# The down products of six routed experts turned round: the weight stays in the array, the 320 slots move, and transposes bring the result back to rows

## The reference, cut to what matters

```
gates = softmax(tokens @ wg); expert_idx = argmax(gates)
capacity = int(1.25 * 2048 / 8)                       # 320
dispatched = einsum('sec,sm->ecm', dispatch, tokens)
h = relu(einsum('ecm,emf->ecf', dispatched, w1) + b1)
expert_out = einsum('ecf,efm->ecm', h, w2) + b2
combined = einsum('sec,ecm->sm', combine, expert_out)
x = layernorm(x + combined)
```

## Time and profile before

| what | us |
|---|---|
| runs, median (lowest to highest) | 1501.31 (1501.03 to 1507.2) |
| the profiled execution, its own time | 1506.99 |
| span of its profile | 1504.9 |
| PE busy in the span | 1416.1 |
| DVE, ACT, POOL busy | 985.0, 878.7, 558.7 |

### The profile page before, as it was taken

How to read it: one execution, slowest core, us unless ns; L and a number is a source line. 1 busy time by engine, 2 the same in 40 slices (tenths; PEclk the granted TensorE clock), 3 DMA queues, 4 the chain that set the end, 5 groups by cost and what they waited for, 6 DMA issues and landing times. The chain is left out here.

```text
span 1504.9 us, 28900 instructions
## 1 busy us (share of the span) xinstructions
PE 1416.1 (94%) x11047; PEld 1070.1 (71%) x11082; DVE 985.0 (65%) x2093; ACT 878.7 (58%) x1442; POOL 558.7 (37%) x727
## 2 busy tenths in 40 slices
PE   6899999999999999999999999999999999867997
PEld 4666666666668888888888888866655555447997
DVE  5677777666664546355444434487678889746896
ACT  1455666766556555464655546455547777636775
POOL 4246865521330121231222202152324444542766
PEclk8999999999989999999999999999999999978999
DMA  7778776662440211202022030245766533105451
GB/s 143 124 143 176 151 158 127 127 108 44 75 63 2 43 30 28 44 8 44 2 43 43 1 51 1 44 79 112 131 159 118 114 79 66 37 32 202 153 173 67
DMA packets 100344, 125.90 MB, mean 84 GB/s; under 512 B 7917, under 2 KB 90356, under 8 KB 97649
## 3 DMA queue, kind: packets, MB, share of 16 engines
q1 hardware_dynamic: 96496, 118.84, 39.6%
q0 software_dynamic: 1984, 4.09, 0.8%
q10 hardware_dynamic: 1728, 1.14, 0.3%
HBM read 50.89 MB, written 9.51 MB: 40 GB/s over the span
## 5 line engine op out<-in xcount | busy, mean ns | idle before, releaser
L958 ACT ACTIVATE probs<-eslot 128x1024 f32<-128x1024 f32 x188 | 192.6, 1025 | 106.9 <-PE eslot L692 103.6
L1187 DVE TENSOR_REDUCE mx<-mslot 128x4 f32<-128x1024 f32 x128 | 156.5, 1223 | 108.9 <-PE mslot L663 107.6
L1489 POOL TENSOR_SCALAR_AFFINE_SELECT probs<-probs 128x512 f32<-128x512 f32 x128 | 83.9, 657 | 348.7 <-ACT probs L956 348.3
L663 PE MATMUL mslot<-stack 48*128 48x256 f32 (+2 forms) x1110 | 163.8, 334 | 17.8 <-DMA stack<-split 12.1
L663 PEld LDWEIGHTS mslot<-stack 48*128 48x128 f32 (+1 forms) x1110 | 97.5, 188 | 104.2 <-issue 87.8
L1181 DVE TENSOR_REDUCE mx_blocks<-mslot 128x3 f32<-128x384 f32 x214 | 114.6, 553 | 62.1 <-PE mslot L663 51.6
L956 ACT ACTIVATE probs<-eslot 128x512 f32<-128x512 f32 (+1 forms) x256 | 111.7, 490 | 50.1 <-PE eslot L692 49.0
L1428 POOL TENSOR_SCALAR ave<-amv 128x2 f32<-128x2 f32 x64 | 22.7, 355 | 301.6 <-DVE amv L1101 260.9
L707 PE MATMUL bank<-probs,v 128*32 128x256 f32 (+1 forms) x2048 | 130.1, 367 | 4.0 <-POOL probs L1489 2.3
L692 PE MATMUL eslot<-stack 50*128 50x256 f32 (+1 forms) x1264 | 124.5, 275 | 4.0 <-ACT probs L958 2.2
L755 PE MATMUL bank<-hidden,l 128*128 128x256 f32 x512 | 114.8, 382 | 0.0
(11 more groups left out here) (269 smaller groups left out, 3512.2 us busy)
## 6 DMA issues: line engine op xcount, KB each, us to landing
stack<-split SPq DMA_DIRECT2D x240, 256.0 KB
w<-in_w SPq DMA_DIRECT2D x16, 1024.0 KB, 6.1
slot_rows<-hTf SPq DMA_DIRECT2D x4, 650.0 KB, 4.6
slot_rows_sb<-slot_rows SPq DMA_DIRECT2D x4, 650.0 KB, 6.2
expert_rows<-slot_rows SPq DMA_DIRECT2D x8, 260.0 KB, 2.7
hT<-in_xT SPq DMA_DIRECT2D x8, 256.0 KB, 8.6
xb<-in_x SPq DMA_DIRECT2D x8, 256.0 KB, 8.7
qk<-in_ctx SPq DMA_DIRECT2D x8, 256.0 KB, 2.9
```

The lines of the kernel that those rows point to most:

```text
L663: mm = pe.matmul(ps[:, first:first + m], queries(u, h, k)[:, qt * P:(qt + 1) * P], keys(u, h, k)[:, 0:m], start=clear, stop=clear or qt == ...
L958: e = act.activation(PR[:, k, :, :, :].rearrange("p a k q -> p (a k q)"), ps[:, :, :, :].rearrange("p a k q -> p (a k q)"), ACT.Exp, scale ...
L1187: dve.tensor_reduce(MX[:, :, :, p].rearrange("p q a -> p a q"), MSLOT[0][:, :, :].rearrange("p a (q k) -> p a q k", q=TT), AX.X, ALU.max)\
L1489: pool.affine_select(diagonal, diagonal, [[0, 2 * TT], [1, P]], ALU.is_ge, 0.0, base=0, channel_multiplier=-1)\
```

## The change

For the experts 1 to 6 (`BY_COLUMN`) the down products are made the other way round. `down_by_column`: for each half `c` of the 256 features the down weight (128 x 128 tiles) is resident and the 320 slots move, 24 matmuls a half, into one of two further PSUM banks (TURN). ScalarE copies each half to `down_T` in SBUF (`down_high`). In the next expert's loop, behind its second up step, PE turns the copy back by 6 transposes into the old banks DOWNS (`down_rows`). Experts 0 and 7 keep the old form. `combine(e, 0..2)` of these six experts moves on VectorE from the end of the loop of e into the loop of e + 1, behind the subtractions of f = 1, 2, 3, and `even(e, 0..2)` behind those of f = 4, 5, 6. The lists of GpSimd and of SyncE stay as they are. The rest of the diff deletes lines in the attention layers that belong to the steps "context high" and "context low", which the plan of steps does not contain, and to projections of layer 1 under `PARTED`, which holds units of layer 0 alone.

```diff
+    down_T = sb("down_T", [P, CC, CAP])
+    BY_COLUMN = range(1, E1 - 1)
 # tensor
+        def down_by_column(e):
+            for c in range(CC):
+                cs = slice(c * P, (c + 1) * P)
+                if e - 1 in BY_COLUMN:
+                    pe.wait_ge(*act_down_T.at(e - 1, c))
+                else:
+                    pe.wait_ge(*dve_rows.at(ST // 2 - 2 + c))
+                for f in range(FC):
+                    if c == 0:
+                        pe.wait_ge(*dve_hid.at(e, f))
+                    mm = products(TURN[c][:, 0:CAP], (w2_high[e % 2][:, f, cs], w2_low[e % 2][:, f, cs]),
+                                  (hid_high[e % 2][:, f, :], hid_low[e % 2][:, f, :]), f == 0, f == FC - 1)
+                mm.then_inc(*pe_down_T(e, c))
+        def down_rows(e):
+            for c in range(CC):
+                pe.wait_ge(*act_down_T.at(e, c))
+            for j, (c0, m) in enumerate(CH):
+                pe.wait_ge(*dve_down.at(e - 1, j))
+                for c in range(CC):
+                    mm = pe.transpose(DOWNS[j][0:m, c * P:(c + 1) * P], down_T[:, c, c0:c0 + m], ident[:, :])
+                mm.then_inc(*pe_down(e, j))
...
+                if e - 1 in BY_COLUMN and f == 1:
+                    down_rows(e - 1)
             pe.wait_ge(*dve_low.at("w2", e))
+            if e in BY_COLUMN:
+                down_by_column(e)
+                continue
 # scalar
+        def down_high(e, c):
+            act.wait_ge(*pe_down_T.at(e, c))
+            if e - 1 in BY_COLUMN:
+                act.wait_ge(*pe_down.at(e - 1, 2))
+            act.activation(down_T[:, c, :], TURN[c][:, 0:CAP], ACT.Copy).then_inc(*act_down_T(e, c))
...
                 weights_high("w1", e + 1)
...
+                if e in BY_COLUMN:
+                    down_high(e, 0)
                 weights_high("w2", e + 1)
+                if e in BY_COLUMN:
+                    down_high(e, 1)
                 gated_bias(e + 1)
 # vector
-                if e >= 1 and f in (1, 3):
+                if e == 1 and f in (1, 3):
                     even(e - 1, (f + 1) // 2)
+                if e - 1 in BY_COLUMN and f in (1, 2, 3):
+                    combine(e - 1, f - 1)
+                if e - 1 in BY_COLUMN and f in (4, 5, 6):
+                    even(e - 1, f - 4)
...
+            if e in BY_COLUMN:
+                weights_low("w2", e + 1)
+                continue
             combine(e, 0)
```

More of the change, by code:

```diff
@@ L101, in build @@
         sb = lambda name, shape: outer.enter_context(nc.sbuf_tensor(name, shape, F32))
[L102 to L105, removed]
+        shared = {"ident": sb("ident", [P, P]), "w1": sb("w1", [P, CC, DFF]), "w2": sb("w2", [P, DFF // P, C]),
+                  "spare": sb("spare", [P, 16 * KEEP])}
         for name in ("w1_in", "w2_in", "biases_in", "scattered", "base_out"):
@@ L279, in attention_layers @@
     HID_A, HID_B = hidden
-    KT_HIGH, KT_LOW = [[shared["context_parts"][:, 2 * k + n, :, :] for k in range(2)] for n in range(2)]
     HID_C = PR[:, 4, :, :, :].rearrange("p a b c -> p (a b) c")
@@ L525, in parts @@
         def parts(u, kind):
-            if u in (PARTED[0], B):
+            if u == PARTED[0]:
                 pe.wait_ge(*dve_step.at("weight low", layer(u), kind))
-            if kind == "q" or layer(u) == 0:
-                return HT_HIGH[u % 2], HT_LOW[u % 2]
-            return KT_HIGH[u % 2], KT_LOW[u % 2]
+            return HT_HIGH[u % 2], HT_LOW[u % 2]
         def project(kind, u, src, co):
@@ L788, in _ @@
                     pe.wait_ge(*act_read.at("T", u))
-                if l == 1 and u in PARTED:
-                    pe.wait_ge(*dve_step.at("context low", u))
                 project("k", u, source(u), 0)
@@ L1001, in _ @@
             elif step == "TC read":
-                if u - 2 in PARTED and u - 2 >= B:
-                    act.wait_ge(*dve_step.at("context low", u - 2))
                 read_turned("TC", u, KT[u % 2], ("g2", "b2"))
@@ L1009, in _ @@
             elif step == "x high" and u in PARTED:
-                act.wait_ge(*(xT_in[u % 2].at(u) if l == 0 else act_read.at("T", u)))
+                act.wait_ge(*xT_in[u % 2].at(u))
                 if u - 2 in PARTED:
-                    act.wait_ge(*bank_filled.at("v" if layer(u - 2) == 0 else "q", u - 2))
+                    act.wait_ge(*bank_filled.at("v", u - 2))
                 act.activation(HT_HIGH[u % 2], HT[u % 2][:, :, :], ACT.Copy).then_inc(*act_step("x high", u))
[L1014 to L1018, removed]
             elif step in ("q read", "k read"):
@@ L1351, in _ @@
                    .then_inc(*dve_step("weight low", l, kind))
-            elif step == "context low" and u in PARTED:
-                dve.wait_ge(*act_step.at("context high", u))
-                dve.tensor_tensor(KT_LOW[u % 2], KT[u % 2], KT_HIGH[u % 2], ALU.subtract).then_inc(*dve_step("context low", u))
             elif step == "logits read":
@@ L1749, in routed_mixture @@
     pe_down = signal("pe_down")
+    pe_down_T = signal("pe_down_T")
+    act_down_T = signal("act_down_T")
     act_rows = signal("act_rows")
```

## The result

The changed kernel takes 1555.83 us, the median of 4 runs (1548.12 to 1558.25), against 1504.26 us for the kernel before in the same comparison: 1.029 times the time, with an interval of 1.0242 to 1.0338. I had said 1547, slower with a chance of 0.92. The profiled execution took 1558.25 us with a span of 1556.5, against 1506.99 and 1504.9.

What follows compares the result with a forecast made beforehand. PE was taken to bound each expert at 15.52 us, a scatter-to-rows chain close behind. Five loops of 24.2 us add 45.2, the tail 1.4: 1501.3 + 46.6 = 1547.9, given as 1547 us, range 1525 to 1560.

Steps and rivals of the forecast that it cites:

- The saving on PE: Down products on PE: 8.48 us become 7.04 plus 0.6 for transposes, saving 0.84 us an expert, 5.0 us for six.
- The loop: Gated bias, relus, combines and evens, scatters, row load, next bias: 20.4 us an expert, 24.2 with splits, against 15.52.
- The idle time of ScalarE before the gated bias: Sign in the changed profile: ScalarE idle 8 to 9 us before gated biases of experts 3 to 7, released by row DMA.
- The splits: VectorE's w1 and w2 splits stall GpSimd's bias instructions by 1.6 and 2.2 us, lengthening the loop from 20.4 to 24.2.
- The first rival: GpSimd's 256-column tensor instructions run beside VectorE's splits, so the loop stays 20.4 us; 1529 us, chance 0.20.
- The tail: Behind expert 7's gated bias, the last expert's second down group starts at 12.3 us instead of 10.9; +1.4 us.
- Expert 2's bias: Gated bias of expert 2 stays as now (1404.97), since its rows wait for expert 0, in the old form.
- The clock rival: PE's clock stays low for much of each loop after idle gaps, adding some 2 us a loop; 1557 us, chance 0.10.
- The rivals with PE in charge: Next expert's rows come before the relus need them, so PE sets the pace: 5.0 us less, 1496.5 us; chance 0.06.
- with no change: A delay just above the 1.5 us reserve eats the 5 us gain; 1501 us, chance 0.04.
- The reserve of the second-longest chain: Slack of the row-load, gated-bias and relu chain behind PE: about 1.5 us an expert; more scatter delay is paid in full.

Runs made afterwards that it cites:

- the run with two bias buffers: Changed kernel with three row buffers, two gated-bias buffers, all roots ahead of the scatters, bias instructions last (first for expert 7); ratio to before 1.001.
- the run with roots first: Changed kernel with three row buffers, bias instructions first on GpSimd and all three roots ahead of the three scatters; ratio to before 1.0007.
- the order-only run: Changed kernel with all down products in the old form, no transposes or copies, combine and even still in the next expert's loop; ratio to before 1.0336.

## Why the prediction was right

**The saving on PE**: 0.84 us an expert was predicted with the transposes at 0.6; they measure 0.65, which leaves 0.79. A half of the down products takes 3.52 us, as the two copies of ScalarE behind them start that far apart (1447.63 and 1451.15), so the 7.04 for both holds. The loop of 14.74 us in the run with two bias buffers fits the whole sum. As foreseen the changed kernel sees nothing of it.

**The loop**, from the start of the gated bias at 1434.84 in the changed kernel: `even(e - 1, 0)` done at 8.1 (foreseen 8.2). First scatter at 8.9 (8.4): a scatter that waits for its even starts 0.8 behind it, not 0.2; the row that I took the 0.2 from did not wait. Third scatter at 18.6 (18.9), the next gated bias at 23.8 (24.2). The mean of the five loops is 23.9. Part of this agreement is luck. In the run with small splits the loop is 20.6 for my 20.4, but its first scatter comes 0.5 us later than I said, and from there to the third it takes 6.3 us for my 6.65. Two errors of some 0.5 and 0.3 us pull in opposite directions. The idle time of ScalarE before the gated bias was also to be 8 to 9 us and is 7.0 to 7.6.

**The splits**: I said that they take 1.6 + 2.2 = 3.8 us from the bias instructions; by experiment it is 3.3 us a loop. The 2.81 us of the earlier trace rows, from which I counted, are not the time of the bias instructions alone; with the splits cut down they take 2.14, so they lose 5.50 - 2.14 = 3.4. Against 2.81 it is 2.7, less than foreseen, as the second of the three got through between the splits and the second split gave way a little. The first rival (1529 us) is refuted by the run with small splits, in which its loop appears only when the splits are gone. The statement of the Trainium skill (GPSIMD Engine Reference, section 1. Specifications) on the interfaces shared with VectorE agrees with this. I used it for GpSimd alone; the run with roots first shows VectorE's subtraction slowed in turn, 1.86 us for 0.48.

**The tail**: +1.4 foreseen, +1.8 found. **Expert 2's bias**: foreseen unchanged, found 2.1 us later in the stage. Its rows took 5.0 us from issue to use where they took 3.0 before; in the order-only run they took 3.3, in the run with the transposes at the expert's end 5.0. It is not the column form as such: in the run with the scatter ahead, which has that form, these rows landed 2.7 us after their issue at the most, for 4.6 in the changed kernel. What slows this one load is open, and was not tried.

**The clock rival** was right that the clock falls (0.50 in a window behind the gap), and wrong in its price: at full clock the loops were no shorter, and the third even came at 11.2 us for 11.1. **The rivals with PE in charge and with no change** failed as their conditions said: the third scatter leaves at 18.6, not at 10.

**The 9 us between 1547 and 1556**: the profiled spans differ from my sum by 1556.5 - 1551.5 = 5.0 us. These are the 2.1 above, 4.1 before the stage, which lies within what this kernel varies by, and 0.4 in the tail, less the 1.6 by which the five loops came out shorter (119.4 for 121.0). Another 3.0 is the median of before, which stood at 1501.3 then and at 1504.3 with one more run, and 0.9 is my step from 1547.9 to 1547. What comes before expert 2's bias I had put at nothing; that the total is still this near is partly luck, as the loops were too long in my sum.

## What to carry to other kernels

Before work is moved behind a wait in a hand-written order, follow the chain from the moved step back to itself: if it goes through a buffer that the next round needs, the move makes a loop, and its length replaces the time of the engine that was to be relieved. The reserve of the second-longest chain (here 1.5 us against a gain of 0.8) is the number to know first. And look at what GpSimd has to do while VectorE runs its long splits: a list that slips by a microsecond or less can fall under one and lose two more.

## What I had not expected of the hardware

- VectorE and GpSimd hold each other up. A GpSimd instruction stalls for about the rest of a split (a root instruction 2.17 us for 0.29, a scatter 2.80 for 1.00). In turn a split grows from 2.29 to 2.75 us and a subtraction from 0.48 to 1.86 beside GpSimd's tensor instructions.
- A tenth of a microsecond decides. A second scatter whose split started 0.56 to 0.58 us behind it took 3.81 us in four kernels (and 6.01 once with the order alone, under both splits); with the split 0.67 to 0.85 us behind it, in the changed kernel, it took 1.60 or 1.61.
- More speed on one engine cost time: with PE at full clock through the gaps, a loop grew by 1 us, since the split of w1 moved onto a scatter.
- With the same instructions up to there, the start of the last stage varies by 15 us in a span of 1500, from kernel to kernel. Differences under 1% had to be read from the stage.
